# Second norm, row halves and turned rows of the first 12 tiles for routing made inside cross-attention, their logits in fp16 halves, and one step without weight pieces

## The reference

```python
# x: (2048, 256) tokens
x = x + attention(layernorm(x))
x = x + cross_attention(layernorm(x), ctx, Wq, Wk, Wv, Wo, gq, gk)   # 16 heads of 128, rmsnorm on q and k
h = layernorm(x)
logits = h @ router_w.T                         # 8 experts
top_v, top_i = top_k(logits, 2)
probs = softmax(top_v)
g, u = h @ gate_w[e].T, h @ up_w[e].T           # 688 wide, for every expert e
x = x + sum over the two chosen e of probs[e] * ((silu(g) * u) @ down_w[e].T)
```

## Time and profile before

| | |
|---|---|
| median of 3 runs | 855.89 us (855.74 to 856.21) |
| profiled execution | 858.77 us, span 856.9 us |
| mean granted TensorE clock | 0.932 |
| busy: PE, DVE, ACT, POOL | 724.8, 572.3, 454.8, 383.9 us |
| from the end of cross-attention to the first expert matmul | 578.5 to 630.3 us |
| moved by DMA | 121.91 MB |

### The profile page before, as it was taken

One profiled execution on the slowest core, in us unless ns is written; L12 is line 12 of the kernel. 1 busy time (PEld: TensorE's weight loads), 2 busy tenths in 40 slices (PEclk: granted clock), 3 DMA queues, 4 the chain that ended last, 5 costly groups with the idle time before them and its releaser, 6 DMA issues. The chain is left out here.

```text
span 856.9 us, 26920 instructions
## 1 busy us (share of the span) xinstructions
PE 724.8 (85%) x10796; PEld 523.9 (61%) x10796; DVE 572.3 (67%) x1060; ACT 454.8 (53%) x875; POOL 383.9 (45%) x446
## 2 busy tenths in 40 slices
PE   0499888887887999999998996989189999999993
PEld 0388777775433556656565665776147777777772
DVE  5768788763886889899989887867853333333330
ACT  0667777754774666666665764544113333333331
POOL 0112222322254555556655556630045666666753
PEclk9879999985997999999999998899589999999998
DMA  9312222311564767566757573619958888988883
GB/s 327 105 50 55 58 55 67 65 52 28 159 192 155 169 132 176 134 173 162 188 125 174 156 180 100 199 52 372 403 89 143 151 147 145 146 135 140 151 142 38
DMA packets 192471, 121.91 MB, mean 142 GB/s; under 512 B 140800, under 2 KB 172800, under 8 KB 192224
## 3 DMA queue, kind: packets, MB, share of 16 engines
q1 hardware_dynamic: 178928, 103.54, 49.9%
q0 software_dynamic: 7488, 9.32, 7.2%
q10 hardware_dynamic: 5936, 7.34, 2.5%
HBM read 61.04 MB, written 27.00 MB: 103 GB/s over the span
## 5 line engine op out<-in xcount | busy, mean ns | idle before, releaser
L1749 DVE SCALAR_TENSOR_TENSOR f_slot_work<-psu,f_slot_work 128x688 f32<-128x688 f32 x39 | 34.1, 874 | 108.8 <-PE psu L1820 108.8
L1345 PE MATMUL xbank_a<-arena,x_o 128*128 128x256 f16 x768 | 97.6, 278 | 4.6 <-DVE x_o L1152 2.6
L1345 PEld LDWEIGHTS xbank_a<-arena,x_o 128*128 128x128 f16 x768 | 74.0, 100 | 27.4 <-DVE x_o L1152 9.1
L1249 PE MATMUL xbank_qk<-arena 128*128 128x512 f16 x336 | 85.2, 391 | 5.6 <-PEq L188 4.3
L1567 POOL DMA_INDIRECT out_dram<-f_y,f_to x39 | 62.2, 1595 | 61.8 <-DMA out_dram<-f_y,f_to 48.0
L1836 PE MATMUL fbank<-arena,f_slot_work 128*128 x663 | 78.9, 273 | 2.6 <-DMA f_slot_work<-hid_hl 2.5
L914 POOL TENSOR_SCALAR arena<-arena 128x512 f32<-128x512 f32 x25 | 37.2, 1489 | 93.7 <-DVE cT L1185 93.7
L1820 PE MATMUL psg<-wgu,f_slot_work 128*128 x468 | 74.7, 309 | 1.9 <-DMA f_slot_work<-rows_in 1.6
L1820 PE MATMUL psu<-wgu,f_slot_work 128*128 x468 | 74.6, 309 | 0.0
L1836 PEld LDWEIGHTS fbank<-arena,f_slot_work 128*128 128x128 f16 x663 | 64.6, 98 | 13.7 <-issue 3.5
L1617 ACT CAST hid_hl<-f_slot_work 128x688 f16<-128x688 f32 x39 | 29.8, 765 | 77.3 <-DVE f_slot_work L1749 73.4
(11 more groups left out here) (285 smaller groups left out, 1703.6 us busy)
## 6 DMA issues: line engine op xcount, KB each, us to landing
arena<-in_wx SPq DMA_DIRECT2D x51, 256.0 KB, 2.9
wgu<-w_hl SPq DMA_DIRECT2D x2, 5504.0 KB, 25.6
ao<-key_norms SPq DMA_DIRECT2D x64, 128.0 KB, 3.4
w_hl<-cT SPq DMA_DIRECT2D x26, 256.0 KB, 2.1
w_hl<-x_pair SPq DMA_DIRECT2D x25, 256.0 KB, 2.2
ao<-in_wx SPq DMA_DIRECT2D x10, 256.0 KB, 3.1
w_hl<-ao SPq DMA_DIRECT2D x10, 256.0 KB, 2.1
x_sb<-in_x SPq DMA_DIRECT2D x4, 512.0 KB, 9.2
```

What stands on the lines that cost most here:

```text
L1249: last = nc.tensor.matmul(query_bank(h), wq[:, a, k, f:f + D2], hT[:, g, b * NCH + k, :], start=(j == 0), stop=(j == len(terms) - 1))
L1345: last = nc.tensor.matmul(acc[t // 2][:, (t % 2) * C:(t % 2 + 1) * C], o_hl[h % 2][:, a, at:at + P], wvo[:, b, e, :], start=(e == 0 and j ...
L1749: nc.vector.scalar_tensor_tensor(out=h3, in0=psu[:, :].rearrange("p (c n) -> p c n", c=2)[:, :, 0:FH], scalar=HID_UP / (H_UP * W_UP), in1= ...
```

## The change

For the first 12 tiles (ROUTED) the second norm, the halves and the turned rows are made within cross-attention, for two tiles at a time (RPAIRS = 6), after their group's residual. `routed_moments` (VectorE) runs in steps 9, 11, 17, 19, 25 and 26; `routed_h` and `routed_high` (ScalarE: norm in place in x_sb by Ln and Exp, and the high halves) at the end of steps 13, 14, 21, 22, 27 and 28; `routed_low` (GpSimd) a step later; and `save_rows` (SP: one store to h_rows and two DMA transposes into the place of x_sb) another step later. The router's weights are loaded, scaled and halved in steps -1 to 1. In `experts` only four tiles are left for statistics, norm, transposes and halves; their norm uses Ln and Exp instead of a square root, the logits of the 12 tiles are 72 fp16 matmuls on the turned rows, the idle matmuls of this part are gone, and the halves' subtraction on VectorE comes after the two best experts are found. No pieces are worked on in step -1 (REST_AT); every later piece comes one step later. `save_group` of the third group moves from step 27 to step 25, ahead of the down weights.

In `cross_attention`:

```diff
+ROUTED = NT - GT
+RPAIRS = ROUTED // 2
...
         def piece_at(N, r):
-            return 2 * (N - first_step) + r
+            if N == REST_AT:
+                return -1
+            return 2 * (N - first_step - (N > REST_AT)) + r
 
...
+        def routed_stats(N):
+            g, r = divmod(N - 1, NU)
+            if g == NG - 1:
+                return [j for j in (RPAIRS - 2 + r,) if r < 2]
+            return [2 * (g - 1) + r // 2] if 1 <= g and r in (0, 2) else []
+
+        def routed_rows(N):
+            g, r = divmod(N - 1, NU)
+            if g == NG - 1:
+                return RPAIRS - 4 + r if 2 <= r < 4 else None
+            return 2 * (g - 1) + r - 4 if 1 <= g and r in (4, 5) else None
+
+        def routed_save(N):
+            return routed_rows(N - 2)
+
+        def hp_of(j):
+            if j % 2 == 0:
+                rows = cT[:, 1]
+            elif j < RPAIRS - 1:
+                rows = hT[:, 1, NCH:2 * NCH, :]
+            else:
+                rows = cT[:, 2]
+            return rows.rearrange("p l n -> p (l n)").rearrange("p (t l c) -> p t l c", t=2, l=2)
+
+        def rows_of(j):
+            return x_sb[:, 2 * j:2 * j + 2, :]
+
...
+                    sp.wait_ge(r_saved[1], (RPAIRS // 2 - 1) * 48)
...
+                def save_rows(j):
+                    sp.wait_ge(r_low_done, j + 1)
+                    sp.dma_start(dram["h_rows"].rearrange("(t p) c -> p t c", p=P)[:, 2 * j:2 * j + 2, :], hp_of(j)[:, :, :, :].rearrange("p t l c -> p t (l c)")).then_inc(r_saved[j % 2], 16)
+                    for a in range(2):
+                        sp.dma_start(x_sb[:, 2 * j + a, :].bitcast(F16).rearrange("p (k n) -> p k n", n=P), hp_of(j)[:, a, :, :].rearrange("p l c -> p (l c)"), transpose=True).then_inc(r_saved[j % 2], 16)
...
-                    if N > 2 and (N - 3) % NU == 0 and 0 < N // NU < NG:
+                    if N == -1:
+                        sp.wait_ge(hT_in, 96)
+                        sp.dma_start(wr[:, :, :], dram["wr"].rearrange("p (k e) -> p k e", k=NCH)).then_inc(wr_in, 16)
+                    if N > 2 and N < TAIL and (N - 3) % NU == 0 and 0 < N // NU:
                         save_group(N // NU - 1)
+                    if N == TAIL + 1:
+                        save_group(NG - 2)
                     if N == TAIL + 2:
                         first_down_weights()
+                    if routed_save(N) is not None:
+                        save_rows(routed_save(N))
...
+                def routed_low(j):
+                    pool.wait_ge(r_high_done, j + 1)
+                    nc.gpsimd.tensor_tensor(hp_of(j)[:, :, 1, :], rows_of(j), hp_of(j)[:, :, 0, :], ALU.subtract).then_inc(r_low_done, 1)
...
+                    if routed_rows(N - 1) is not None:
+                        routed_low(routed_rows(N - 1))
...
+                def routed_h(j):
+                    part = slice(2 * j, 2 * j + 2)
+                    act.wait_ge(r_stats_done, 2 * j + 2)
+                    routed.step(nc.scalar.mul(r_minus[:, part], r_mv[:, part, 0], -1.0))
+                    routed.link(nc.scalar.activation(r_ln[:, part], r_mv[:, part, 1], ACT.Ln, bias=cst[:, CONSTS:CONSTS + 1]))
+                    nc.scalar.activation(r_rstd[:, part], r_ln[:, part], ACT.Exp, scale=-0.5, bias=cst[:, CONSTS + 6:CONSTS + 7]).then_inc(r_norm_done, 1)
+                    act.wait_ge(r_norm_done, j + 1)
+                    for t in (2 * j, 2 * j + 1):
+                        nc.scalar.mul(r_minus[:, t:t + 1], r_minus[:, t:t + 1], r_rstd[:, t:t + 1]).then_inc(r_shift_done, 1)
+                    act.wait_ge(group_saved, (j // 2 + 1) * 16)
+                    act.wait_ge(r_shift_done, 2 * j + 2)
+                    for a in range(2):
+                        t = 2 * j + a
+                        nc.scalar.activation(rows_of(j)[:, a, :], x_sb[:, t, :], ACT.Identity, scale=r_rstd[:, t:t + 1], bias=r_minus[:, t:t + 1]).then_inc(r_rows_done, 1)
+
+                def routed_high(j):
+                    act.wait_ge(r_rows_done, 2 * j + 2)
+                    if j >= 2:
+                        act.wait_ge(r_saved[j % 2], j // 2 * 48)
+                    nc.scalar.copy(hp_of(j)[:, :, 0, :], rows_of(j)).then_inc(r_high_done, 1)
...
+                    if routed_rows(N) is not None:
+                        routed_h(routed_rows(N))
+                        routed_high(routed_rows(N))
+                    if N == 0:
+                        act.wait_ge(wr_in, 16)
+                        nc.scalar.mul(wr[:, :, :], wr[:, :, :], W_UP).then_inc(wr_ready, 1)
+                        act.wait_ge(wr_ready, 1)
+                        nc.scalar.copy(wr_hl[:, 0], wr[:, :, :]).then_inc(wr_ready, 1)
...
+                def routed_moments(j):
+                    dve.wait_ge(x_done, j // 2 * 2 + j % 2 + 1)
+                    for a in range(2):
+                        routed.step(nc.vector.bn_stats(r_stats[:, a, :], x_sb[:, 2 * j + a, :]))
+                    routed.settle()
+                    for a in range(2):
+                        nc.vector.bn_aggr(r_mv[:, 2 * j + a, :], r_stats[:, a, :]).then_inc(r_stats_done, 1)
...
+                    for j in routed_stats(N):
+                        routed_moments(j)
```

In `experts`:

```diff
+                for u in range(GT // 2):
+                    pair = slice(2 * u, 2 * u + 2)
+                    act.wait_ge(s["stats_ready"], 2 * u + 2)
+                    links.link(nc.scalar.activation(root[:, pair], mv[:, pair, 1], ACT.Ln, bias=cst[:, CONSTS:CONSTS + 1]))
+                    nc.scalar.activation(rstd[:, pair], root[:, pair], ACT.Exp, scale=-0.5, bias=cst[:, CONSTS + 6:CONSTS + 7]).then_inc(s["roots_ready"], 1)
+                act.wait_ge(s["wr_in"], 16)
...
-                    nc.scalar.copy(hTf[u % 2][:, :, :, :].rearrange("p a k n -> p (a k n)"), ps[u % 2][:, :]).then_inc(s["t_copied"], 1)
-                    nc.scalar.copy(hp[:, 2 * u:2 * u + 2, 0:C], ao[:, 2 * u:2 * u + 2, :]).then_inc(s["hh_ready"], 1)
...
+                    nc.scalar.copy(hTf[u][:, :, :, :].rearrange("p a k n -> p (a k n)"), ps[u][:, :]).then_inc(s["t_copied"], 1)
+                for u in range(GT // 2):
+                    nc.scalar.copy(hp[:, 2 * u:2 * u + 2, 0:C], ao[:, ROUTED + 2 * u:ROUTED + 2 * u + 2, :]).then_inc(s["hh_ready"], 1)
+
+                act.wait_ge(s["hl_ready"], GT // 2)
+                act.dma_start(dram["h_rows"].rearrange("(t p) c -> p t c", p=P)[:, ROUTED:, :], hp[:, :, :]).then_inc(s["h_saved"], 16)
...
-                token_stats(nc, c, x_sb, stats, mv)
-                dve.sem_inc(s["stats_ready"], 1)
-                dve.wait_ge(s["roots_ready"], 1)
-                c.link(nc.vector.reciprocal(rstd[:, :], root[:, :]))
-                c.link(nc.vector.tensor_scalar(rstd[:, :], rstd[:, :], H_UP, None, ALU.mult))
-                for t in range(NT):
-                    nc.vector.tensor_scalar(ao[:, t, :], x_sb[:, t, :], mv[:, t, 0:1], rstd[:, t:t + 1], ALU.subtract, ALU.mult).then_inc(s["h_ready"], 1)
-                dve.wait_ge(s["h_ready"], NT)
-                for u in range(NT // 2):
-                    dve.wait_ge(s["hh_ready"], u + 1)
-                    nc.vector.tensor_tensor(hp[:, 2 * u:2 * u + 2, C:2 * C], ao[:, 2 * u:2 * u + 2, :], hp[:, 2 * u:2 * u + 2, 0:C], ALU.subtract).then_inc(s["hl_ready"], 1)
...
-                dve.wait_ge(s["l_done"], NT // 2)
+                for u in range(GT // 2):
+                    for a in (2 * u, 2 * u + 1):
+                        c.step(nc.vector.bn_stats(stats[:, a, :], x_sb[:, ROUTED + a, :]))
+                    c.settle()
+                    for a in (2 * u, 2 * u + 1):
+                        nc.vector.bn_aggr(mv[:, a, :], stats[:, a, :]).then_inc(s["stats_ready"], 1)
+                for u in range(GT // 2):
+                    dve.wait_ge(s["roots_ready"], u + 1)
+                    dve.wait_ge(s["stats_ready"], 2 * u + 2)
+                    for a in (2 * u, 2 * u + 1):
+                        nc.vector.tensor_scalar(ao[:, ROUTED + a, :], x_sb[:, ROUTED + a, :], mv[:, a, 0:1], rstd[:, a:a + 1], ALU.subtract, ALU.mult).then_inc(s["h_ready"], 1)
+                dve.wait_ge(s["h_ready"], GT)
...
+                for u in range(GT // 2):
+                    dve.wait_ge(s["hh_ready"], u + 1)
+                    nc.vector.tensor_tensor(hp[:, 2 * u:2 * u + 2, C:2 * C], ao[:, ROUTED + 2 * u:ROUTED + 2 * u + 2, :], hp[:, 2 * u:2 * u + 2, 0:C], ALU.subtract).then_inc(s["hl_ready"], 1)
...
-                dve.wait_ge(s["hl_ready"], NT // 2)
...
-                idle_work(ps[3], 32)
-                pe.wait_ge(s["wr_in"], 16)
...
-                        last.then_inc(s["l_done"], 1)
+                for t in range(ROUTED):
+                    terms = [(k, a, b) for k in range(NCH) for a, b in ((0, 0), (0, 1), (1, 0))]
+                    turned = x_sb[:, t, :].bitcast(F16).rearrange("p (l k n) -> p l k n", l=2, k=NCH)
+                    for j, (k, a, b) in enumerate(terms):
```

(28 more changed lines are left out.)

75 lines of the change are left out of this document (37 added, 38 removed).

## The result

The changed kernel takes **866.0 us** (median of 4 runs, 865.28 to 868.08) beside 855.82 for the kernel before on the same chip: a ratio of 1.0119 (95% interval 1.0088 to 1.0149), 7.5 to 12.8 us slower. The forecast was 857.5 and its range ended at 865. The profiled execution took 866.51 us, with a span of 864.6.

The account below looks back on a forecast made before the run. TensorE bounds cross-attention, a chain of small steps routing, TensorE then scatters the expert slots. Terms -5.5 - 11 + 2 + 8.2 + 8 = +1.7 us on 855.89 gave 857.5 us, range 846 to 865.

Parts of the forecast that it names:

- B: Routing: with 12 of 16 tiles gone from the block, the first expert matmul comes earlier; gain 11 us, bounds 9 and 15.
- E: Tail, steps 24 to 32: later pieces 3, moments 1, ScalarE blocks 4; loss 8 us, bounds 2 and 13.
- A: Steps -1 and 0: without pieces in step -1, the wait for the logs goes; gain 5.5 us, bounds 3 and 7.3.
- C: Cross-attention's full steps: routed moments on VectorE, four times, cost 0.5 us each; loss 2 us, bounds 0 and 4.2.
- D: Steps 14, 15, 22, 23: norm and halves in ScalarE blocks delay TensorE; loss 8.2 us, bounds 0 and 11.4.
- R3: Routing: the weights don't hold the slots up, so its gain is 15 us; 853.5 us, chance 0.13.
- R1: Cross-attention and tail: ScalarE's gaps take the blocks, costing 0 and 1 us there; 846.4 us, chance 0.25.
- R2: Tail: TensorE's clock falls twice more after new waits, some 2.5 us each time; 862.5 us, chance 0.17.

Follow-up runs that it names:

- e3: Changed kernel with ScalarE's norm of the 12 tiles left out and the high-half copy cut to 2 columns; 855.4 us, ratio 0.9999.
- e14: Changed kernel without loading the last four experts' down weights, their place set to zero by GpSimd; 868.9 us, ratio 1.0210.
- e5: Changed kernel with GpSimd's low half at the head of its step and the last down weights issued after the first slot's rows; 861.4 us, ratio 1.0064.
- e2: Kernel before with only the step without weight pieces added (later pieces one step later); 852.3 us, ratio 0.9978.
- e12: Kernel before with only the step without weight pieces, run once more in more rounds; 856.3 us, ratio 0.9993.
- e6: e5 with ScalarE's block for two routed tiles cut in three and placed where ScalarE waits for TensorE; 848.6 us, ratio 0.9934.
- e8: Changed kernel with only ScalarE's block cut in three and placed where ScalarE waits for TensorE; 855.5 us, ratio 0.9992.

## Why the prediction was wrong

Over both profiles of each kernel the stages differ by +4.9 us (steps), +9.6 (tail) and -6.7 (routing), +7.8 in sum; the timed runs say 7.5 to 12.8. The forecast had +4.7, +8 and -11. Of the 6.1 us between +7.8 and its +1.7, B makes 4.3 and E 1.6.

- **A, C and D held.** Steps -1 and 0 fell by 5.4 us on the mean of two profiles each (5.5 forecast; the usual value is nearer 4, above). Steps 10, 12, 18 and 20 grew by 1.9 (2 forecast), with and without ScalarE's blocks; no run leaves the moments themselves out. Steps 14, 15, 22 and 23 grew by 8.2 (8.2 forecast), and e3 shows that ScalarE's blocks did it.
- **B is the step that failed:** "The turns of the first rows stand behind them in the SP queue and take 2.7 us, so the first expert matmul comes at 616 to 621". The logits, the gate/up weights' end (the SP queue is nearly done at 630, 36 us after the block's start; forecast 34.4) and the end of all bytes (634, 40.3 us; forecast 40.1) came about as worked out. But the first gather and turn were priced from the old trace, where the DMA had run dry under them. Now they came while the ACT queue's down weights still filled the engines: 6.13 and 4.90 us. And TensorE, idle for that long, began slot 0 at the lower clock, a term that the sum did not have. Both together cost up to 8.1 us by e14; without them B would have come near the 15 of R3. In the stage that holds both, B gave 6.7 us, not 11. The rule of the Trainium skill ("DMA: Bandwidth & Descriptors", Issuing engines are not separate DMA queues) says that DMAs of several issuers interleave on the same 16 engines. The trace agrees: the gather took 6.13 us beside the ACT queue's loads, and 3.1 in e5, where these come later. That the gain of 9, which the forecast took from the rule, lies near the 8.5 us by which the first expert matmul came earlier is luck: it let gate/up land with the last byte, but gate/up was nearly through at 630, and the turned rows set the start at 636.98.
- **E missed a third of its term.** Blocks: 4 forecast, 4.6 measured (e3). Pieces: 3 forecast, 2.1 measured (e2, e12). The moments (1 forecast) don't show: e6 has them, and its tail of 46.4 is that of e2 and e12 (46.7 and 46.6), which have none. So the other 2.9 of 9.6 us are what the forecast put at nothing: "SP's save and two transposes, some 1.75 us of issue, stand right behind turn_p and 3 us ahead of the next piece's save". In step 24 there is no `turn_p`, and the low half comes behind GpSimd's extra quotient, so the save held the pieces. By the tails that order costs 2 us (e5 against the changed kernel) to 5 (e8 against e6). I had looked at SyncE's room in a full step and not in the first step of the tail.
- **R1 was right about ScalarE's gaps and wrong about the place.** They take the whole block (e6) if its parts stand ahead of instructions that wait anyway; at the end of the step, ahead of `out_high`, 8.2 of the four blocks' 11.8 us reached TensorE. **R2** came in part: step 25 ran at a granted 0.60 (0.69 before) and step 28 at 0.82 (1.00 before), and both steps hold waits for the turned copy (5.75 and 2.27 us).
- About 2 us between the stages' +7.8 and the median's +10.2 remain open; they are within the interval.
- Three small readings were off and change nothing: 0.68 us for 8 matmuls are 85 ns each, not 88; 855.89 + 1.7 is 857.6, not 857.5; and cross-attention's first matmul starts at 210 us, not 217.

## What to carry to other kernels

Here a block of 2.95 us on ScalarE, which is idle a third of the time, cost TensorE up to 2.5 us where the next instruction was due, and nothing measurable when its parts stood ahead of instructions that wait: place moved work by the rows that carry a wait, cut as small as these waits. Price a transfer that comes earlier by what the queues move at its new time, not by its row at the old one, and add the lower clock of an engine that will have idled for it. When a wait is put on a queue, follow it in every kind of step, the first and last ones above all.

## What the runs showed of the hardware

In e14 GpSimd cleared 3072 and then 9216 fp16 columns (the places of one and of three experts) in 10.53 us from 593.76 on, and VectorE's four normalised tiles, which take 1.51 us in the changed kernel, took 9.77 beside it. One of them alone took 7.94 us: it began 0.13 us after the second clearing and ended 0.14 us after that one's end (timelines of GpSimd and VectorE in e14, and of VectorE in the changed kernel):

```profile
596.36 7.93 POOL L1649 MEMSET arena<- 128x9216 f16 x1
```

```profile
596.49 7.94 DVE L1756 TENSOR_SCALAR ao<-x_sb,f_mv,f_rstd 128x256 f32<-128x256 f32 x1
```

```profile
595.59 1.51 DVE L1760 TENSOR_SCALAR ao<-x_sb,f_mv,f_rstd 128x256 f32<-128x256 f32 x4
```

So an instruction of GpSimd can hold one of VectorE up until it ends; the Trainium skill ("SBUF — State Buffer", SBUF: two separate sides) describes this as an exclusive lock on a shared pair of ports, and the row agrees. These 8.3 us are why e14's routing did not get shorter.

While both queues have work, they move about as many packets, and not as many bytes. In the changed kernel's routing this shows from 614 to 618 (DMA view, queues: packets, MB, share; q1 is the SP queue, q10 the ACT queue):

```profile
q1 hardware_dynamic: 257, 1.41, 84.7%
q10 hardware_dynamic: 257, 0.26, 18.5%
```

From 621 to 624 they moved 159 and 157 packets, but 0.88 and 0.41 MB. So the down weights, which come in the smaller packets, moved slowly as long as the SP queue had work, and were still coming when the first gather was issued.
